# Moving the eighth shared expert ahead of the expert pairs

## The reference

```python
x = layernorm(x + attention(x))     # linear attention, 16 heads, gated
x = layernorm(x + ffn(x))

# ffn, on tokens of width 256
weights, indices = gate(x)          # 16 experts in 4 groups: best 2 groups, then best 4 experts
c[token, expert] = weights          # zero for the experts not taken
h1, h3 = x @ w1[e], x @ w3[e]       # 256 -> 128, for each expert
y = sum_e c[:, e] * ((silu(h1) * h3) @ w2[e])
z = (silu(x @ ws1) * (x @ ws3)) @ ws2   # the shared expert, 256 -> 256 -> 256, every token
ffn = y + z
```

## Time and profile before

| | us |
|---|---|
| median of 3 runs (lowest, highest) | 562.92 (561.91, 564.67) |
| the profiled execution, its own time | 563.45 |
| its span | 561.6 |
| TensorE busy | 457.2 (81%) |
| VectorE busy | 395.1 (70%) |
| ScalarE busy | 291.8 (52%) |
| GpSimd busy | 293.1 (52%) |

### The profile page before, as it was taken

How to read it: one execution, slowest core, us unless ns; L and a number is a source line. 1 busy time by engine, 2 the same in 40 slices (tenths; PEclk the granted TensorE clock), 3 DMA queues, 4 the chain that set the end, 5 groups by cost and what they waited for, 6 DMA issues and landing times.

```text
span 561.6 us, 12184 instructions
## 1 busy us (share of the span) xinstructions
PE 457.2 (81%) x3189; PEld 320.5 (57%) x3213; DVE 395.1 (70%) x1147; ACT 291.8 (52%) x627; POOL 293.1 (52%) x334
## 2 busy tenths in 40 slices
PE   1599979794979796976995899899889899898930
PEld 1145636442546454543553789789777777787620
DVE  1454686874685764667687677668979989888754
ACT  3154564544462634361221477676766776777621
POOL 1001010578767676765774000057778787777771
PEclk9999999997999997987998999999999999999985
DMA  8121314364433121222753477699999999898651
GB/s 210 53 63 51 95 36 114 83 207 144 151 111 107 64 103 67 103 76 104 253 213 114 124 220 211 199 250 305 302 279 305 274 332 316 275 313 292 193 201 50
DMA packets 55012, 97.74 MB, mean 174 GB/s; under 512 B 8752, under 2 KB 22080, under 8 KB 54976
## 3 DMA queue, kind: packets, MB, share of 16 engines
q1 hardware_dynamic: 29472, 38.56, 23.3%
q0 software_dynamic: 12288, 33.57, 19.3%
q10 hardware_dynamic: 13216, 25.17, 12.1%
HBM read 50.88 MB, written 46.40 MB: 173 GB/s over the span
## 4 chain that ended last, share of the span: by engine, by line
PE 37%; DVE 21%; DMA 12%; issue 11%; POOL 8%; ACT 7%; ACTq 1%; SPq 1%; DVEq 1%; POOLq 0%
DMA wa_stage<-expert_out,result_of 5%; POOL expert_in L391 4%; PE h_even L1142 3%; PE h_odd L1142 3%; PE h_even L1144 3%; PE h_odd L1144 3%; PE h_odd L1143 3%; DMA q_fm<-expert_out,result_of 3%; DVE x_all L1096 3%; PE h_even L1143 3%; DMA expert_out<-k_exp 3%; PE h_even L1188 2%; PE t L1367 2%; ACT x_all L490 2%; PE t L1149 2%
## 5 line engine op out<-in xcount | busy, mean ns | idle before, releaser
L391 POOL DMA_INDIRECT expert_in<-x_all,slots x128 | 133.2, 1041 | 45.7 <-issue 35.8
L416 POOL DMA_INDIRECT wa_stage<-expert_out,result_of x64 | 63.9, 998 | 19.1 <-issue 14.2
L416 POOL DMA_INDIRECT q_fm<-expert_out,result_of x32 | 31.5, 984 | 76.1 <-DMA expert_out<-k_exp 66.9
L377 POOL TENSOR_SCALAR neg_mean<-mv 128x4 f32<-128x4 f32 x16 | 5.3, 329 | 109.3 <-DVE mv L714 109.0
L645 ACT ACTIVATE wa_hi<-bias_heads 128x256 f16<-128x256 f32 x80 | 33.2, 415 | 33.5 <-DVE bias_heads L1079 33.0
L1367 PE MATMUL t<-ident,kv 128*128 128x128 f32 x320 | 48.1, 273 | 1.6 <-DVE xsT_lo L1068 1.6
L1068 DVE TENSOR_TENSOR xsT_lo<-t,xsT_hi 128x512 bf16<-128x512 f32 x60 | 41.0, 684 | 11.8 <-ACT xsT_hi L597 11.0
L597 ACT ACTIVATE xsT_hi<-t 128x512 f16<-128x512 f32 x60 | 35.5, 593 | 24.4 <-PE t L1367 12.2
L1143 PE MATMUL h_even<-xsT_lo,we_hi 128*128 128x256 bf16 x160 | 43.6, 273 | 0.0
L1142 PE MATMUL h_even<-xsT_hi,we_hi 128*128 128x256 f16 x160 | 43.6, 273 | 0.0
L1144 PE MATMUL h_even<-xsT_hi,we_lo 128*128 128x256 f16 x160 | 43.6, 273 | 0.0
(11 more groups left out here) (231 smaller groups left out, 1435.3 us busy)
## 6 DMA issues: line engine op xcount, KB each, us to landing
kv<-expert_in SPq DMA_DIRECT2D x80, 256.0 KB, 4.6
expert_out<-k_exp ACTq DMA_DIRECT2D x40, 256.0 KB
expert_out<-q_exp ACTq DMA_DIRECT2D x40, 256.0 KB
stage<-in_L_ffn_w SPq DMA_DIRECT2D x48, 128.0 KB
expert_in<-wa_stage SPq DMA_DIRECT2D x17, 256.0 KB
x_in<-in_L_attn_x SPq DMA_DIRECT2D x8, 512.0 KB, 4.3
out<-gated ACTq DMA_DIRECT2D x8, 512.0 KB, 4.3
expert_in<-x_all,slots POOLq DMA_INDIRECT x128, 2.4
```

Source lines behind the costliest of these rows:

```text
L391: pool.indirect_dma_start(xs_dram, bass.IndirectOffsetOnAxis(ap=slots[:, b, t, j:j + 1], axis=0), x_all[:, b, t, :], None).then_inc(dispat ...
L416: pool.indirect_dma_start(y_got[i][:, j, :], None, ys_dram[0:pairs_until(k) * PAIR, :], bass.IndirectOffsetOnAxis(ap=result_of[:, b, t, j: ...
```

## The change

`EARLY` becomes 8. All eight shared experts then run in stage 2, and everything that was written for the eighth in the tail is taken out. Three things follow from the constant without a line of their own: the loop `for n in range(4, EARLY)` in the VectorE list has one more round, and with three parts behind each half it reaches all 24 parts of `place_results`; the side jobs of the pairs then begin with `weigh_slots` at pair 0; TensorE, ScalarE and GpSimd run their shared loops to g = 15.

```diff
-    EARLY = NB - 1
+    EARLY = NB
@@ ScalarE, behind the last pair
             store_out(b)
-            for g in range(SHARED * EARLY, SHARED * NB):
-                shared(g)
             for n in range(b + 1, NB):
@@ VectorE, behind the last pair
             two_groups(GROUPS_OF_PAIRS - 2, summed - 1, last=True)
-            for g in range(SHARED * EARLY, SHARED * NB):
-                shared_hidden(g)
-            add_shared(EARLY)
-            dve.wait_ge(shared_added, NB)
             for b in range(summed, NB):
@@ TensorE, behind the last pair
             chunks = two_groups(GROUPS_OF_PAIRS - 2, last=True)
-            pe.wait_ge(pair_a_ready, NPAIR - 1)
-            up(SHARED * EARLY, EARLY, 0)
             for i in range(2):
                 down_pair(NPAIR - 2 + i, RING - 2 + i, chunks[i])
-            pe.wait_ge(pair_a_ready, NPAIR)
-            up(SHARED * EARLY + 1, EARLY, 1)
-            pe.wait_ge(ys_copied, NPAIR)
-            for n in range(EARLY + 1, NB):
-                up(SHARED * n, n, 0)
-                up(SHARED * n + 1, n, 1)
-                down(n - 1)
-            down(NB - 1)
```

## The result

The changed kernel took 572.25 us, the median of four runs (571.34 to 572.93), against 563.79 us of the kernel before beside it (561.91 to 567.88, four runs). The ratio is 1.0139, with a 95% interval of 1.0079 to 1.0199: slower by 1.4%. The profiled execution took 571.34 us with a span of 569.8; before it was 563.45 with 561.6, so 7.9 us more. The forecast was 6.7 us more (569.6 from a median of 562.92, range 565.0 to 573.5).

What follows compares the result with a forecast made beforehand. VectorE bounds the shared stage, TensorE the first pairs, then GpSimd's gather stream. Span 561.6 + 9.0 (front) - 2.3 (tail) = 568.3; against the median, 562.92 + 6.7 = 569.6 us, range 565.0 to 573.5.

Steps and rivals of the forecast that it cites:

- What bounds the kernel: From the first gather on, GpSimd's 128 gathers set the pace, waiting only for their own issue, 0.56 us at longest.
- The tail gives back 2.3: At the end, tile 31's sums start when its last gather lands, 549.0 instead of 551.35, so 2.3 us come back.
- The rival with 12.7 us: In the tail, all the shared expert took comes back, 12.7 us against 9.0 in front: 559.2; chance 0.05.
- the rival with a late landing: In the tail, the last gather lands 4.8 to 5.8 us after issue, nothing given back: 572 to 573; chance 0.12.
- 12.9 us from the last issue to the end: At the end, the kernel finishes 12.9 us behind the last gather's issue and not 15.2.
- The front, 9.0: Ahead of the pairs, the last add_shared comes 9.0 us later: 9.2 in the sum, less overlaps.
- The halves and parts: VectorE's work before add_shared(6): halves 14 and 15, 3.98 us, and parts 18 to 23, 3.91, together 7.89.
- down(7), charged like down(6) of before: TensorE's last down product ahead of the pairs, charged 4.26 us and not 2.62, after some 5.8 us idle.
- The reason given for the low clock: In the shared stage, down(6) ran at half clock, 0.50 for 3.00 us, after TensorE stood idle 4.15 us.
- The rival with the low clock throughout: Ahead of the pairs, TensorE is at half clock throughout, front 13.5 us, net 11.2: 574.1; chance 0.09.
- The parts beside the pairs come back at 0: Removing 3.91 us of side jobs from pairs 0 to 5 gains 0; bounds 1.4 and -0.3, as TensorE bounds them.
- The stream keeps its length: From the first gather on nothing changes: same 128 gathers by 1.25 us and same norms, only later.

Runs made afterwards that it cites:

- e5: The changed kernel with only the last of four GpSimd instructions left in each of seven norms between gathers; 563.10 us against 564.56 before, ratio 0.9978.
- e3: The kernel before, eighth expert still in the tail, with only placing parts 18 to 23 moved ahead of the pairs, behind half 13; 567.51 us, ratio 1.0081.
- e1: The kernel before with the shared expert of batch 7 not computed at all; 562.38 against 563.85 us, ratio 0.9975.
- e4: The changed kernel with 26 unread matmuls on TensorE between down(6) and down(7); 570.11 us, ratio 1.0124 to the kernel before.
- f1: The changed kernel itself again, with more runs beside the kernel before; 571.09 against 564.40 us, ratio 1.0131.
- e2: The changed kernel with placing parts 18 to 23 kept beside pairs 0 to 5; 566.96 us, ratio 1.0052 to the kernel before.
- e7: The changed kernel with the changes of e2 and e4 together, but 13 unread matmuls; 567.29 against 564.56 us before, ratio 1.0049.
- f2: The changed kernel with batch 6's norm done behind tile 31's gathers; 570.28 against 564.40 us before, ratio 1.0111.
- e6: The kernel before with the first two instructions of each norm at the end moved from GpSimd to VectorE; 561.45 against 564.56 us, ratio 0.9950.
- f3: The changed kernel with the changes of e7 (8 matmuls, not 13), e6 and f2 together; 560.14 against 564.40 us before, ratio 0.9929.

## Why the prediction was right, and where its sizes were off

- *What bounds the kernel.* The stream of gathers held its place in every kernel: in all thirteen traces the first is 57.2 to 57.3 us behind the last sum ahead of the pairs, and e5 shortened the stream through GpSimd's instructions alone. Right, but with little to spare: in the changed kernel one gather stands 0.84 us for a store, and in e3 one 1.19 for a product, where the prediction had 0.56 as the longest.
- *The tail gives back 2.3.* 2.19 by the traces, and 1.5 by the times of e1. The rival with 12.7 us is refuted by e1. The landing: in the changed kernel the DMA engines are silent from 558.5 on, at most 2.5 us behind the last issue, so the rival with a late landing (5.83 us) is out. In all kernels without the expert in the tail tile 31's sums start 2.7 to 2.9 us behind the last issue. The sign "12.9 us from the last issue to the end" was missed: it is 13.8 (15.2 before), as the last store took longer (below).
- *The front, 9.0.* 9.64. The halves and parts took 7.67 where the sum had 7.89. The term that was mis-sized is down(7), charged like down(6) of before: on TensorE it took 4.91 us and not 4.13, since nearly all of it ran at the low clock, and `add_shared(6)` to `add_shared(7)` was 6.61 and not 5.83. The sum has a slip there: 316.12 + 0.14 + 4.26 is 320.52, and its 320.66 needs 4.40, which is what lay between the start of down(6) and `add_shared(6)`; the 9.2 is right by that. The reason given for the low clock was weaker than it looked, as in the earlier trace rows it had fallen to 0.51 ahead of the stand, in down(5); e4 is what shows that down(7) runs at full clock without a stand. The rival with the low clock throughout did not come in this trace: both up and down(6) ran at full clock. In f1's trace up(14) began at the low clock, and TensorE's slack ahead of `add_shared(6)` took it up (its front is 9.6 too).
- *The parts beside the pairs come back at 0.* Confirmed from both sides by e2 and e3, and by 38.91 against 38.96 us for pairs 0 to 16.
- *The stream keeps its length.* 179.56 and not 177.65. With the same gathers and norms it was 179.21 in f1, 178.81 in e4, 179.54 in e2 and 180.51 in e7, and without the change 178.55 in e1 and 179.71 in e3. It scatters by some 2 us also with the expert in the tail, and the profiled execution of before lay at the short end. That is no effect of the change that can be shown. Most of the 1.9 us lies in gathers of over 1.0 us: 37 of them in the changed kernel (5.8 us over 0.95 in sum), 27 before (4.2), and 37 (5.6) in e1.
- *The rest.* `add_shared(5)` came 2 us sooner than before, and the last store took 4.0 us from its issue to the end in place of 3.2. Neither was forecast, and no run tells their cause. The 2 us are there at `add_shared(0)` already (255.16 and not 257.12), behind a stretch that the change leaves as it was; in the thirteen traces that sum starts between 254.60 and 257.74. The store took 3.7 to 4.0 in f1, f2, e2, e4 and e7 too, and 3.2 in the others.

The sum was 6.7, the medians say 6.7 (f1) and 8.5 (first set), with intervals that hold both. The mechanism was right; that f1 comes out at 6.7 to the tenth is luck. By the traces the front was 0.6 us over the forecast, the stream 1.9 and the end 0.8, and the start of the kernel 2.0 under it.

## What to carry to other kernels

Where two chains end almost together, taking the longer one away wins only the difference: here 2 us of 12.7. Look for the engine that pauses only for its own issue, and see what its first instruction waits for; here all that was put ahead of that start was paid nearly in full, while the same VectorE work beside pairs that TensorE bounds was free. What is left to win is in the stream itself, down to the small instructions between its DMAs; and once it is shorter, what the other chain costs has to be measured again: 2 us became 4.5.

## What was not expected of the hardware

- Stands of TensorE cost differently, and not by their length. After 2.61 us (e2) the down product began at full clock, fell within it and took 3.8 us; after 4.15 us (before) and after 9.35 us (e3) it took 4.1; after 6.09 us (the changed kernel) and 4.93 us (f1) 4.9, almost all at the low level; with the stand filled (e4) 2.6. The Trainium skill's "TensorE: Matmul & The Clock Gate", section "What's actually happening", has two states only. The windows agree: those that lie within one level show 0.50 or 1.00, and values between, as 0.52 here, come where the level changes inside the window.
- The first gather behind a norm of four GpSimd instructions took 1.07 to 1.24 us before (1.07 to 1.33 over all traces), behind one of two instructions 1.00 to 1.06 in e6 (one of 1.27 in f3); most others take 0.95.
